# The causal mask of the maxima: four half-height products, or one full-height product a bank behind the values

## What is computed

```python
B, T, D, NH, HD, HID = 4, 512, 256, 16, 16, 704
xn = layernorm(x)
q, k, v = (xn @ W.T split into 16 heads, for W in Wq, Wk, Wv)
att = q @ k.T / sqrt(16) + triu(full((T, T), finfo.min), k=1)
s = (softmax(att) @ v, heads joined) @ Wo.T
W = (wq - 128) * scale[:, None]              # gate, up, down
g = silu((silu(xn @ Wgate.T) * (xn @ Wup.T)) @ Wdown.T)
out = x + s * g
```

## Time and profile before

| | us |
|---|---|
| median of 3 runs | 377.93 |
| lowest, highest | 376.08, 378.49 |
| the profiled execution | 376.7 |
| its span, first to last instruction | 374.9 |
| PE, DVE, ACT, POOL busy | 310.1, 218.4, 168.6, 121.4 |

### The profile page before, as it was taken

One profiled execution on the slowest core, in us unless ns is written; L12 is line 12 of the kernel. 1 busy time (PEld: TensorE's weight loads), 2 busy tenths in 40 slices (PEclk: granted clock), 3 DMA queues, 4 the chain that ended last, 5 costly groups with the idle time before them and its releaser, 6 DMA issues.

```text
span 374.9 us, 5717 instructions
## 1 busy us (share of the span) xinstructions
PE 310.1 (83%) x2192; PEld 199.3 (53%) x2192; DVE 218.4 (58%) x362; ACT 168.6 (45%) x238; POOL 121.4 (32%) x183
## 2 busy tenths in 40 slices
PE   0184096779987999899999998999999999998755
PEld 0162073466654655476665554666666667564323
DVE  4762078654545599755646898637456555557212
ACT  2311163234433556445426566534346665435730
POOL 4600065321113354521014646301126564112310
PEclk9999679869998999999999999999999999999996
DMA  7628790010397500120879101005793010001101
GB/s 280 160 72 186 182 166 2 3 56 3 106 170 203 88 1 3 25 92 14 203 189 197 23 0 58 2 4 155 172 231 64 0 60 3 1 3 56 59 0 56
DMA packets 21038, 31.40 MB, mean 84 GB/s; under 512 B 2308, under 2 KB 9988, under 8 KB 21012
## 3 DMA queue, kind: packets, MB, share of 16 engines
q1 hardware_dynamic: 20740, 30.26, 33.7%
q10 hardware_dynamic: 272, 0.79, 0.6%
HBM read 20.19 MB, written 10.49 MB: 82 GB/s over the span
## 4 chain that ended last, share of the span: by engine, by line
PE 51%; DVE 23%; DMA 13%; ACT 5%; issue 3%; SPq 3%; POOL 0%; POOLq 0%; DVEq 0%; ACTq 0%
PE ps L307 11%; DMA qk_scratch<-hid 10%; PE ps L309 9%; PE ps L308 8%; PE ps L462 7%; PE ps L408 5%; PE ps L443 5%; DVE mx L851 4%; DVE mx L853 3%; PE ps L420 3%; DMA qp<-ctr 2%; DVE nw L816 2%; DVE xn L823 2%; DVE hid L839 2%; ACT hid L586 2%
## 5 line engine op out<-in xcount | busy, mean ns | idle before, releaser
L762 POOL TENSOR_SCALAR_AFFINE_SELECT pt<-pt 128x256 f32<-128x256 f32 (+1 forms) x112 | 48.5, 447 | 145.1 <-ACT pt L640 145.1
L640 ACT ACTIVATE pt<-ps 128x1024 f32<-128x1024 f32 x80 | 81.9, 1024 | 27.5 <-PE ps L443 27.4
L307 PE MATMUL ps<-xh,guh 128*128 128x512 f32 x96 | 43.6, 454 | 14.3 <-DVE hid L839 10.0
L408 PE MATMUL ps<-kp,qp 48*128 48x512 f32 (+3 forms) x256 | 37.4, 350 | 14.4 <-DVE mx L851 8.2
L851 DVE TENSOR_REDUCE mx<-ps 128x2 f32<-128x1024 f32 x32 | 39.1, 1222 | 13.0 <-PE ps L420 12.5
L748 POOL TENSOR_TENSOR hl<-hid,hh 128x512 fp32r<-128x512 f32 x24 | 32.0, 1332 | 42.2 <-ACT hh L600 41.8
L462 PE MATMUL ps<-pt,vt 128*17 128x256 f32 (+3 forms) x512 | 44.6, 444 | 0.8 <-POOL pt L762 0.8
L443 PE MATMUL ps<-qp,kp 50*128 50x512 f32 (+3 forms) x256 | 40.7, 375 | 4.9 <-ACT pt L640 2.4
L744 POOL TENSOR_TENSOR hid<-hid 128x512 f32<-128x512 f32 x24 | 30.7, 1278 | 43.2 <-DVE hid L839 27.2
L586 ACT ACTIVATE hid<-ps,hsg 128x512 f32<-128x512 f32 x24 | 16.5, 689 | 52.2 <-PE ps L309 33.0
L308 PE MATMUL ps<-xl,guh 128*128 128x512 f32 x96 | 38.6, 402 | 0.0
(11 more groups left out here) (96 smaller groups left out, 525.8 us busy)
## 6 DMA issues: line engine op xcount, KB each, us to landing
qk_scratch<-hid SPq DMA_DIRECT2D x32, 256.0 KB
qp<-qk_scratch SPq DMA_DIRECT2D x16, 256.0 KB, 5.0
kp<-qk_scratch SPq DMA_DIRECT2D x16, 256.0 KB, 6.3
qp<-qk_scratch SPq DMA_DIRECT2D x16, 128.0 KB, 5.8
kp<-qk_scratch SPq DMA_DIRECT2D x16, 128.0 KB, 7.1
xr<-in_x SPq DMA_DIRECT2D x4, 512.0 KB, 3.6
out<-xr SPq DMA_DIRECT2D x8, 256.0 KB, 2.6
xin<-in_x SPq DMA_DIRECT2D x3, 512.0 KB, 3.5
```

Of the source, the lines that this page charges most:

```text
L307: nc.tensor.matmul(dst, lh, rh, start=start, stop=False)
L408: nc.tensor.matmul(ps[:, MX + e, c:c + w], qp[part, place(b, half), col, i * P:(i + 1) * P], kp[part, place(b, half), col, 0:w], start=(z ...
L640: nc.scalar.activation(pt[:, 2 * kk:2 * kk + 2, :], ps[:, ST:ST + 2, :], ACT.Exp, scale=SCALE).then_inc(exp_done, 1)
L762: mm = nc.gpsimd.affine_select(out=diag, in_=diag, compare_op=ALU.is_ge, fill=0.0, base=0, pattern=[[0, diag.shape[1]], [1, P]], channel_m ...
```

## The change

The two constants `rows2` and `tri2`, in halves, give way to a full 128 x 128 identity `identb` and one triangle `tri`, both bf16. The mask becomes one product a bank over all 128 rows, two a step instead of four. It moves out of `maxima` into a function `diagonal`, which now signals `sm_ready`, and is issued in each step behind the step's values and ahead of its other units; where a step has no values it is issued directly behind the products. In the head it follows each `maxima` directly. No wait is added; the first maxima's wait on `consts` counts to 3 instead of 2. POOL makes the constants with three fills and three selects instead of five and nine.

```diff
-                for r in range(2):
-                    for e in range(2):
-                        part = slice(64 * e, 64 * e + 64)
-                        bank = ps[:, MX + e, :]
-                        if kk < 2:
-                            dst, tri = bank[:, 3 * P:], tri2[part, r, :]
-                        else:
-                            dst = (bank[:, 2 * P:].rearrange("p (a n) -> p a n", a=2) if kk < 4 else
-                                   bank.rearrange("p (a b n) -> p a b n", a=2, b=2)[:, :, 1, :])
-                            tri = tri2[part, r:r + 1, :].to_broadcast([64, 2, P])
-                        mm = nc.tensor.matmul(dst, rows2[part, r, :], tri, start=False, stop=(r == 1))
+
+            def diagonal(b, m):
+
+                kk = m % 5
+                for e in range(2):
+                    bank = ps[:, MX + e, :]
+                    if kk < 2:
+                        dst, mask = bank[:, 3 * P:], tri[:]
+                    else:
+                        dst = (bank[:, 2 * P:].rearrange("p (a n) -> p a n", a=2) if kk < 4 else
+                               bank.rearrange("p (a b n) -> p a b n", a=2, b=2)[:, :, 1, :])
+                        mask = tri[:].rearrange("p (a n) -> p a n", a=1).to_broadcast([P, 2, P])
+                    mm = nc.tensor.matmul(dst, identb[:], mask, start=False, stop=True)
                 mm.then_inc(sm_ready, 1)
...
                 if n >= 6:
                     maxima(0, n - 6)
+                    diagonal(0, n - 6)
...
-            maxima(0, 6)
-            maxima(0, 7)
+            for m in range(6, LEAD):
+                maxima(0, m)
+                diagonal(0, m)
             for b in range(B):
                 for s in range(STEPS):
                     scores(b, s)
-                    if STEPS * b + s + LEAD < STEPS * B:
-                        maxima(*divmod(STEPS * b + s + LEAD, STEPS))
-                    for kind, of, n in step_units(b, s):
-                        unit(kind, of, n)
+                    ahead = STEPS * b + s + LEAD
+                    if ahead < STEPS * B:
+                        maxima(*divmod(ahead, STEPS))
+                    units = step_units(b, s)
+                    for kind, of, n in units:
+                        if kind == "pv" and ahead < STEPS * B:
+                            unit(kind, of, n)
+                    if ahead < STEPS * B:
+                        diagonal(*divmod(ahead, STEPS))
+                    for kind, of, n in units:
+                        if kind != "pv" or ahead >= STEPS * B:
+                            unit(kind, of, n)
```

More of the change, by code:

```diff
@@ L137, in build @@
         ident = sb("ident", [P, P])
-        rows2 = sb("rows2", [P, 2, P], BF16)
-        tri2 = sb("tri2", [P, 2, P], BF16)
+        identb = sb("identb", [P, P], BF16)
+        tri = sb("tri", [P, P], BF16)
         cn = sb("cn", [P, P])
@@ L398, in maxima @@
                 if n == 0:
-                    pe.wait_ge(consts, 2)
+                    pe.wait_ge(consts, 3)
                 else:
@@ L701, in _ @@
             nc.gpsimd.memset(ident[:], 0.0).then_inc(pool_step, 1)
[L702 to L705, removed]
+            nc.gpsimd.memset(identb[:], 0.0).then_inc(pool_step, 1)
+            nc.gpsimd.memset(tri[:], 0.0).then_inc(pool_step, 1)
             nc.gpsimd.memset(u[0:8].rearrange("p a k n -> p (a k n)")[:, 0:3 * T], 1.0).then_inc(ones_set, 1)
-            pool.wait_ge(pool_step, 5)
+            pool.wait_ge(pool_step, 3)
@@ L708, in _ @@
             nc.gpsimd.affine_select(out=ident[:], in_=ident[:], compare_op=ALU.not_equal, fill=1.0, base=0,
                                     pattern=[[-1, P]], channel_multiplier=1).then_inc(consts, 1)
[L713 to L723, removed]
-                                        pattern=[[1, 64]], channel_multiplier=-1).then_inc(pool_step, 1)
@@ L725, in _ @@
-            pool.wait_ge(pool_step, 13)
-            nc.gpsimd.nop().then_inc(consts, 1)
+            nc.gpsimd.affine_select(out=identb[:], in_=identb[:], compare_op=ALU.not_equal, fill=1.0, base=0,
+                                    pattern=[[-1, P]], channel_multiplier=1).then_inc(consts, 1)
+            nc.gpsimd.affine_select(out=tri[:], in_=tri[:], compare_op=ALU.is_ge, fill=NEG, base=0,
+                                    pattern=[[-1, P]], channel_multiplier=1).then_inc(consts, 1)
             for w in range(2):
```

## The result

| | before | after |
|---|---|---|
| median, beside the first runs | 377.0 (375.5 to 378.5, 4 runs) | 385.2 (382.5 to 386.8, 4 runs) |
| median, measured again later | 378.2 (377.0 to 380.1, 11 runs) | 385.3 (380.6 to 387.3, 6 runs) |
| the profiled execution, its span | 376.7, 374.9 | 382.5, 380.7 |
| mean granted clock of PE, median of the later runs | 0.950 | 0.939 |

The ratio to the kernel before is 1.021 (95% interval 1.013 to 1.029) in the first measurement and 1.012 (1.007 to 1.018) in the second. It counts only runs within 1.5% of a kernel's fastest, which is why it is smaller than the ratio of the second pair of medians; this kernel scatters over nearly 7 us, and a good part of this study is about why.

The account below looks back on a forecast made before the run. The bound was taken to vary by stage: PE's own work, or its waits for the DVE's reductions. Losses 3.3 + 2.7 + 0.7 = 6.7 less gain 2.4 gave 4.3 on 377.9: 382.2 us, range 378 to 388.

Parts of the forecast that it names:

- The late reductions: Steps with values alone: reduction starts later, uncovered; 1.09 us at step 0 of items 1 to 3, more in item 3.
- the steps with a unit behind the values: The unit covers the reduction's lateness of 0 to 1.1 us before the next maxima, so cost 0.
- The c row: Item 3, step 11: the last reduction, feeding shift row c through a DMA, comes later and costs 0.7 us.
- Queued work on the DVE: chunk_lo, gate, residual and finish behind a late reduction become ready after its new end anyway: cost 0.
- Steps 4, 8 and 9: Short steps of item 3: 0.1 us each, by the switch or lateness just over the room.
- The saving: Where PE's work sets the time, full-height masks behind the values gain 0.05 us at 47 maxima: 2.4 us, bounds -0.9 and 3.8.
- The rule of the Trainium skill: If only the count of tiling-mode switches decides, full-height masks gain nothing where a full-height unit follows: 384.6 us.
- The head: Before the step loop, the switch and bf16 weight load lie inside four rounds where PE waits: 0.7 us lost.
- rival (c): PE's clock falls to half for 7.0 us at step 0 of items 1 to 3: 392.7 us, one item 385.7; chance 0.11.
- Rival (a): Smaller loss at step 0 and item 3, full saving of 3.8 us: 380.1 us, chance 0.21.
- (b): Faster: PE catches up behind each step 0 of items 1 to 3, absorbing the stalls: 376.9 us, chance 0.06.
- (d): The mask's place is hidden throughout and only weight loads change: 375.5 us, chance 0.05.

Follow-up runs that it names:

- a2: The changed kernel measured again with nothing altered, profiled a second time: 385.3 us median of six runs.
- e1: The kernel before with full-height masks in their old place, straight behind the maxima's products: 382.1 us, ratio 1.009.
- e3: The change, but the mask goes first in steps with values alone or no unit: 377.9 us, ratio 1.003.
- e5: e3 plus zero products in PE's waits in head and tail: 373.9 us, ratio 0.986 to the kernel before.
- e6: The kernel before plus zero products in PE's waits in head and tail: 372.6 us, ratio 0.986.
- e8: The change, with the mask ahead of the values only in step 0 of every item: 381.9 us.
- e10: The change plus zero products in head and tail and 24 more in its new waits: 377.8 us, ratio 0.9995 to the kernel before.
- e7: The change, with the mask ahead of the values only in steps 3, 9, 10 and 11 of item 3: 381.9 us.

## Why the prediction was right, and where it was not

The direction and the range held: 382.2 forecast, 385.2 measured, inside 378 to 388, though the centre was 3 us low. That it was no further off is in part luck: the mechanism came out 1.2 us smaller than the sum, and the clock, which the sum took as unchanged, added on the other side.

**The late reductions: right, step by step.** 1.09 us at each step 0 was forecast, 1.08, 1.07 and 1.12 came; 0.6 and 1.1 at steps 3 and 10 of item 3, 0.60 and 1.07 came. That the steps with a unit behind the values pay nothing was right as well: in items 1 and 2, step 0 apart, only the round of step 9 of item 1 grew by more than 0.1 us (0.21), it holds no values, and it differs from trace to trace (0.72 in a2, 0.00 in e1).

**The c row: nearly.** 0.7 forecast, 0.52 measured.

**Queued work on the DVE at nothing: wrong for one place.** I costed the residual behind a late reduction at zero, since its own input comes later. In item 3, step 8, the reduction is 0.6 late, the residuals follow it back to back, and the next reduction, ready at 344.28 (0.43 behind the mask), starts at 344.47 behind them:

```profile
343.28 1.28 DVE L913 TENSOR_TENSOR xr<-ps,xr 128x512 f32<-128x512 f32 x2
...
343.85 0.39 PE L422 MATMUL ps<-tri,identb 128*128 128x256 bf16 x2
...
344.47 0.95 DVE L850 TENSOR_REDUCE mx<-ps 128x2 f32<-128x768 f32 x1
```

Steps 4, 8 and 9 cost 0.56 instead of 0.3.

**The saving: its sign and place right, its size a little low.** What no row of before could show was how much of the bf16 weight load lies open. It lies hidden altogether:

```profile
276.99 0.39 PE L422 MATMUL ps<-tri,identb 128*128 128x256 bf16 x2
277.14 0.47 PE L307 MATMUL ps<-xh,guh 128*128 128x512 f32 x1
...
277.45 0.39 PE L308 MATMUL ps<-xl,guh 128*128 128x512 f32 x1
```

This is the step of the earlier trace rows. From the first mask product to the unit's second it is 0.46 us, where I had 0.03 + 0.24 + 0.24 = 0.51 and the kernel before 0.66, less the switch now ahead (0.09: a mask product of full height starts 0.15 us behind a maxima's product of 128 columns, one of half height 0.06). Where PE sets the pace, most steps with 256 columns gained 0.05 to 0.15 each, most of those with 128 columns 0.03 to 0.08 (0.07 and 0.02 forecast); step 2 of items 1 and 2 lost 0.09. All other steps together gained 2.9 us, not 2.4. The rule of the Trainium skill (TensorEngine Tiling (Array Packing), section Key Properties) that a change of tiling mode drains the engine was not the whole price: at an equal number of switches the order of what stands behind them was worth up to 0.15 us each. No median shows this saving: e3, which keeps nearly all of it, is level with the kernel before, and e5 is behind e6.

**The head: too high.** 0.7 forecast; in the second profile of the change and in e8, which lack the extra fall at 61.6 us, it was 0.1 to 0.3.

**The clock: the term that was missing.** The sum took the clock as it was, and rival (c) had 0.11 with a fall of 7 us in each item or in one. The sum without the clock came out at 3.1, lower than the 4.3 forecast, and the medians hold 4 to 5 us more, which I put down to the clock; the filled waits of e10 and the grants bear out a part. That waits following each other bring falls was rightly named, but the place was not the step 0 of items 1 to 3, where no profile of the change shows one: the falls are at the end of item 3, in the head and in the tail, and the one at the end of item 3 begins behind waits of 0.38 and 0.68 us, ahead of the late masks of steps 10 and 11. I also reckoned with a fall or none, and it is a matter of chance from run to run, which is why the medians show it more than any one profile. The page TensorE: Matmul & The Clock Gate of the Trainium skill, section Why this matters for your kernels, warns against idle gaps between bursts of products. The traces agree in part: the long fall of a2 begins behind waits of 0.38 and 0.68 us, but the same two waits stand in the first profile of the change without a fall. My row of 1.00 from 160 to 254 us only spoke for a stretch where PE hardly waits. Rival (a) fell, since no saving was near 3.8; (b) fell, since the traces show the 1.1 us of each step 0 carried on, less the savings: item 1 as a whole is 0.31 us longer, and step 9 of item 2, beside the reload of q and k, is 0.30 us shorter in the change and 0.40 in e1, which has no late masks; (d) fell with the first row of L850.

Still open: in which runs the clock falls, and which of the waits bring it. e7 and e8 each removed half of the late masks and got back no grant at all in the medians of six runs; e10 filled six waits at once, among them one ahead of step 10, and got back 4 us, so it doesn't tell the late masks from the two waits ahead of step 10. Only one profile stands for each kernel, so the places in the other runs were not seen.

## What to carry to other kernels

Before moving an instruction behind other work of its engine, list every step in which that other work is alone: the cover must stand behind the moved instruction, and a rule that is right in 66 of 72 steps can lose all in the other six. By the rows, a mask or correction of full height gains where it takes the first place behind a switch of tile shape, since its bf16 weights load unseen and the next float32 product follows at the steady pace (0.46 us against 0.66); the gain was up to 0.15 us a step, and too small to show in a median here. A new wait on TensorE has a second price, the clock: compare the granted clock of several runs, not of one profile, and try products of zero in the waits; here they came with 5.6 us less in the median of a kernel that was otherwise unchanged.

## What the hardware showed that I had not expected

- Products with a zero stationary matrix count as activity: with 28 of them in head and tail the grant from 71 to 86 us rose from 0.66 to 1.00 and the median fell from 378.2 to 372.6 us.
- Even without any change the time follows the clock: of 70 runs of the kernel before (375.5 to 381.8 us), the 20 with a mean grant of up to 0.949 have a median of 379.0 us, the 16 with more than 0.955 one of 376.7.
- Two waits of 0.38 and 0.68 us within 1.6 us stood ahead of a fall of the clock in some executions (a2: half clock from 345.0 us for 10.2; mean grant 0.68 from 340 to 356 us) and not in others (the first profile of the change: 1.00 from 345 to 361 us).
